# Where the clearing transfers of the experts' input stand in SP's queue of a graph-network kernel

## The reference

```python
cnt = cnt.at[dst, edge_type].add(1.0)
inv_deg = 1.0 / jnp.maximum(cnt[dst, edge_type], 1.0)
for l in range(DEPTH):                       # 4
    h = jnp.einsum('ni,rio->rno', X, W)
    msg = h[etype, src] * inv_deg[:, None]
    agg = jax.ops.segment_sum(msg, dst, num_segments=X.shape[0])
    out = agg + X @ root + bias
    ...
    X = jax.nn.elu(layernorm(out)) + X
...
top_vals, top_idx = jax.lax.top_k(logits, K) # K = 2 of 8 experts
```

## Time and profile before

| | |
|---|---|
| time, median of 3 runs | 2591.7 us (2585.16 to 2593.56) |
| the profiled execution's own time | 2582.19 us |
| its span in the trace | 2580.4 us |
| PE busy | 2099.1 us (81%) |
| DVE, ACT, POOL busy | 1564.4, 825.1, 1251.7 us |
| mean granted TensorE clock | 0.911 of full |
| DMA moved | 443.95 MB, mean 172 GB/s |

### The profile page before, as it was taken

The page is one execution under the profiler, slowest core; times in us unless marked ns, Lnnn a source line. Parts: engine busy times, 40 slices in busy tenths (PEclk is TensorE's granted clock), DMA queues, the critical chain, the costliest instruction groups (busy, mean ns, idle before and its releaser), DMA issues. The chain is left out here.

```text
span 2580.4 us, 46242 instructions
## 1 busy us (share of the span) xinstructions
PE 2099.1 (81%) x16341; PEld 1303.8 (51%) x16341; DVE 1564.4 (61%) x4433; ACT 825.1 (32%) x1679; POOL 1251.7 (49%) x1223
## 2 busy tenths in 40 slices
PE   2667788888789898989889888888897988774993
PEld 1334455555454454555545555555453554444992
DVE  7957666666575465666545565665364665565665
ACT  3645545445365111111111211111010111113992
POOL 2055443353510366666526666663656666642441
PEclk6688899899899999999989999999998999886997
DMA  6798343343433587676547877665775656532335
GB/s 150 176 289 249 122 132 108 111 133 116 126 89 130 185 238 227 216 220 193 180 123 260 236 235 221 213 213 171 223 228 162 179 174 179 152 94 64 93 96 178
DMA packets 211689, 443.95 MB, mean 172 GB/s; under 512 B 40881, under 2 KB 137150, under 8 KB 209795
## 3 DMA queue, kind: packets, MB, share of 16 engines
q1 hardware_dynamic: 138291, 273.04, 34.6%
q0 software_dynamic: 61408, 156.79, 20.6%
q10 hardware_dynamic: 11760, 11.08, 1.7%
HBM read 336.54 MB, written 103.89 MB: 171 GB/s over the span
## 5 line engine op out<-in xcount | busy, mean ns | idle before, releaser
L1446 POOL DMA_INDIRECT n_BIG<-n_xd,n_SIDX x1080 | 1111.2, 1029 | 1093.6 <-PE n_PS L1931 453.2
L1912 PE MATMUL n_PS<-n_BIG 125*128 125x500 f16 x4800 | 1187.7, 386 | 60.9 <-issue 33.9
L1912 PEld LDWEIGHTS n_PS<-n_BIG 125*128 125x128 f16 x4800 | 439.6, 100 | 500.4 <-issue 128.8
L1931 PEld LDWEIGHTS n_PS<-n_OW,n_BIG 128*128 128x128 f16 x4320 | 256.5, 99 | 198.3 <-issue 67.9
L1931 PE MATMUL n_PS<-n_OW,n_BIG 128*128 128x84 f16 (+21 forms) x4320 | 305.9, 202 | 53.2 <-issue 45.6
L1951 PE MATMUL n_PS<-n_BIG,n_tabs 128*128 128x256 f16 x2400 | 310.9, 284 | 32.8 <-issue 30.9
L1626 DVE TENSOR_TENSOR n_ST<-n_PS,n_INVB 128x500 f32<-128x500 f32 x200 | 200.2, 1043 | 158.8 <-remote 62.8
L1951 PEld LDWEIGHTS n_PS<-n_BIG,n_tabs 128*128 128x128 f16 x2400 | 243.3, 102 | 85.5 <-issue 48.6
L1652 DVE SCALAR_TENSOR_TENSOR n_U<-n_PS,n_cw,n_BI 125x256 f32<-125x256 f32 x100 | 48.3, 483 | 350.0 <-remote 194.7
L1337 ACT ACTIVATE n_tabs<-n_ST 128x1000 f16<-128x1000 f32 x100 | 103.8, 1038 | 383.8 <-DVE n_ST L1626 263.9
L1321 ACT ACTIVATE n_BIG<-n_PS 128x500 f16<-128x500 f32 x300 | 163.5, 577 | 189.5 <-PE n_PS L1883 122.6
(11 more groups left out here) (276 smaller groups left out, 2268.7 us busy)
## 6 DMA issues: line engine op xcount, KB each, us to landing
n_BIG<-n_a SPq DMA_DIRECT2D x175, 625.0 KB
n_a<-n_BIG SPq DMA_DIRECT2D x12, 3125.0 KB
n_xg<-n_tabs SPq DMA_DIRECT2D x53, 481.9 KB
n_INVB<-n_ind SPq DMA_DIRECT2D x100, 250.0 KB
n_BIG<-n_xd,n_SIDX POOLq DMA_INDIRECT x1080
n_BIG<-in_L_ffn_W_dram SPq DMA_DIRECT2D x32, 512.0 KB
n_xd<-n_BIG SPq DMA_DIRECT2D x75, 112.0 KB
n_whl<-n_BIG SPq DMA_DIRECT2D x16, 512.0 KB
```

What stands on the lines that cost most here:

```text
L1446: e.indirect_dma_start(m.GR[:, g % GS, :], None, m.XD[l % 2][:, :], bass.IndirectOffsetOnAxis(ap=m.SIDX[:, i:i + 1], axis=0)).then_inc(s[f ...
L1912: ins = e.matmul(m.bank(2 * p + h, 0, W), m.xps[l % 2][0:TN, part, D * k + 128 * h:D * k + 128 * h + 128], m.RA[0:TN, c.slot_of(n), W * (k ...
L1931: ins = e.matmul(m.bank(2 * p + h, at, c.width[q]), m.GR[:, g % GS, D * part + 128 * h:D * part + 128 * h + 128], ow, start=(first == 0 an ...
```

## The change

The 54 clearing transfers keep their size and their waits. Before, transfer n stands in SP's queue behind block n, so that all 54 stand behind blocks 0 to 53. Now transfer k stands behind block 50 + 4k, the first behind tile 1's last blocks, the last behind block 262 of 300.

```diff
--- before.py
+++ after.py
@@ -50,6 +50,7 @@
 ZROWS = 96
 ZN = 5
 N_ZERO = math.ceil((DUMMY + 128) / ZROWS / ZN)
+ZERO_FROM, ZERO_STEP = 50, 4
 ROWS = (0, 112), (112, TN)
 HEAD = 32
 SIGMA = 4.0
@@ -341,8 +342,8 @@
                 split_in[l] = run("dve", 3.0, run("act", 2.6)) + 0.3
             elif what == "block":
                 unit_ready["block", n] = run("act", 0.6) + 0.2
-                if n < N_ZERO:
-                    order.append(("zx", 0, n))
+                if n >= ZERO_FROM and (n - ZERO_FROM) % ZERO_STEP == 0 and (n - ZERO_FROM) // ZERO_STEP < N_ZERO:
+                    order.append(("zx", 0, (n - ZERO_FROM) // ZERO_STEP))
             elif what == "tile":
                 job(time["pe"] + 5.0, "degree", 0, n)
             elif what == "counts":
```

## The result

The changed kernel takes 2575.64 us (median of 8 runs, 2568.62 to 2587.94) where the kernel before takes 2589.61 us on the same chip (8 runs, 2585.16 to 2600.48). The ratio is 0.9949, with a 95% interval of 0.993 to 0.9968 (some 8 to 18 us): 14.0 us less, where 15.5 was forecast. The profiled execution took 2569.7 us, 12.5 less than the profiled one of before.

What follows compares the result with a forecast made beforehand. DVE sets the pace while tile 0 is built, then PE, which idles 13.88 us for tile 0's counts. Terms -13.9 - 1.2 - 1.4 + 1.0 = -15.5 us take the median from 2591.7 to 2576.2; range 2566 to 2588.

Steps and rivals of the forecast that it cites:

- Tile 0's counts: At PE's start on tile 0's degrees: the 13.88 us wait for the counts' transfer goes entirely, -13.9 us.
- Both delays of the counts: Before tile 0's degrees: 6.5 us in SP's queue, some 7.6 us behind bytes already handed to the DMA engines.
- What is late next: Behind tile 0's counts: DVE doesn't become the bound; POOL's gathers count nothing, with 5 us as far end.
- The clock: At the 16 products behind tile 0's degrees: 3.70 us at full clock instead of 4.90, -1.2 us.
- The late inverse: At 231 to 243 us, DVE's 3.37 us wait for an inverse goes; -1.4 us taken, bounds 0 and 3.4.
- Other idle time: PE from 160 to 215 us, 22% idle under DMA load: 0 us taken as gain, 3.3 kept as bound.
- The clears in their new place: From about 200 to 765 us, clears delay small transfers behind them in SP's queue: +1 us, bounds 0 and 8.
- a sign of its being wrong: PE's waits for counts, inverses or gathered rows appearing between 200 and 760 us would show the prediction wrong.
- Slower: Rival: clears in their new place delay what stands behind them, up to 93 us, unhidden; 2606 with a third; chance 0.04.
- The counts still land late: Rival: x's last halves and POOL's first gathers delay tile 0's counts instead of the clears; 2584 us, chance 0.12.
- More comes back: Rival: all bounds on the gaining side at once, 21.8 us, giving 2570 us; chance 0.08.
- The forecast DMA share of 0.57: From 240 to 760 us, the moved clears raise the DMA engines' share from 0.41 to 0.57.

Runs made afterwards that it cites:

- e3: The kernel before, with tile 0's counts sent from ACT's queue instead of SP's and all clears in their old place; ratio 1.0 to the kernel before.
- e5: The kernel before, unchanged, run once more on a chip where it takes 2277 us; one run, 2281.01 us.
- e12: The kernel before with 25 clears left behind blocks 0 to 24, the other 29 behind every fourth block from 50; ratio 1.0008 to the kernel before.
- e7: The changed kernel with all 54 clears behind blocks 246 to 299, one per block; ratio 1.0068 to the kernel before.
- e1: The changed kernel itself again, on a chip where the kernel before takes 2280 us; ratio 0.9869 to the kernel before.
- e2: The changed kernel with the clears behind blocks 25 to 78, one per block, beside tile 1; ratio 1.006 to the kernel before.
- e11: The changed kernel itself once more, on a chip where the kernel before takes 2280 us; ratio 0.9846 to the kernel before.
- e9: The changed kernel plus 54 transfers of 24.7 KB in the clears' old places; ratio 0.9866 to the kernel before.

## Why the prediction was right, and where it was not

- *Tile 0's counts, -13.9.* It measured 12.1 at D. The wait went entirely, but PE came 1.8 us later than assumed: 0.9 us later to the 12 products before, which then took 3.68 us instead of 2.69, at a granted clock of 0.75 (133 to 137 us; before 1.00). Both delays of the counts are real: past SP's queue D comes at 139.49 (e3) instead of 150.39 (e5), and the 7.3 us that the counts then take to land leave 3.17 us of wait. That this term gives the gain by itself is shown on no chip. e3 has it alone and gets 1.0; e12 leaves it out and gets 1.0008, which shows that it is needed on that chip, not that it is enough.
- *What is late next.* The prediction asked this, and named DVE's own work and POOL's gathers. The answer in e3 is the inverses, 15.47 and 17.05 us of DVE's waits. The sum was spared this only because the change moves the clears away from the inverses as well.
- *The clock, -1.2.* The 16 products took 3.54 us instead of 4.90, 1.4 less; the 12 products before them gave 1.0 back.
- *The late inverse, -1.4.* DVE's wait of 3.37 us is gone, and yet the lead over before, 13.5 us at the first gathered rows, is 9.2 at M, where the sum has it rise. 4.3 us are lost in between; one trace of each kernel on a chip with stops can't say to what. The bound of 3.4 was the mistake in method: it is the wait for the inverse that is left behind late counts, not what the inverse costs once the counts are early.
- *Other idle time, 0 with 3.3 as bound.* Nothing shows against it on the chip of the forecast (e12, and the window of 160 to 215 us). Elsewhere it is the largest mistake: DVE's 20.0 us for inverses in e5. The step that failed there is "No row of PE there names a transfer, so I take 0". PE's row names DVE, and DVE waits for the transfer; rows of SP with 12 clears in 20.63 us between two inverses were there to follow.
- *The clears in their new place, +1, bounds 0 and 8.* One wait of 1.47 us for tile 2's counts shows, between 200 and 760 us, where the prediction had put a sign of its being wrong. The lead of 9.2 us at M is 9.9 at the degrees of tile 11 (816.32 against 826.23), behind the last clear, so no larger loss is seen. On the faster chips e7 against e1 puts it at about 8. The forecast DMA share of 0.57 came out at 0.54.
- *The rivals.* "Slower" had a true mechanism, 1.68 us a clear, wherever clears stand in a row (e2, e7); the change keeps them four blocks apart in the list. "The counts still land late" did not come: behind early halves and gathers they were there in time. "More comes back", 21.8 us at most, was too small for the other chips, where e1 and e11 gained 31 to 35.

The time was forecast within 1.5 us, and some of that is luck. At the end of layer 0 the two traces stand 9.9 us apart, at their ends 12.5 (the last 2.6 where the change moves nothing), the medians 14.0 with an interval of 8 to 18. What the prediction had right is that the clears make the counts late in two ways, that this goes entirely, and that the clears cost little where they now stand. What it had wrong is that the counts are the gain: they are one of two delays, and early counts alone give nothing where that was tried (e3).

## What to carry to other kernels

Bulk transfers that nobody waits for still set the pace of small ones that somebody waits for; put them where the DMA engines are idle, or apart by more than their own time, and never in a row close ahead of a small one. Removing one late transfer of a row moves the wait to the next, so follow each releaser over a second and third hop and ask when the next hop would be ready if the first were early. The wait that the trace shows at the second hop is only what the first has left of it. And the same change was worth 14 us on one chip and 31 to 35 on two others, so compare within one chip, and say of which kind it was.

## What was not expected of the hardware

- The same kernel takes 2277 to 2280 us on three chips and 2586 to 2590 in two sets, at mean granted clocks of 0.934 and 0.911 for the profiled kernel before. For the changed kernel 199 of 321 us are idle time of PE, with 207 us of its waits put down to "issue" against 2; DVE is busy for as long (1565.4 and 1560.7 us). The cause stays open.
- A store of 2 KB on ACT's own queue took 10.2 us to land while SP's clears filled the DMA engines, and 2.1 us without them.
- SP issues a single clear in 0.42 us, with idle DMA engines (276.33 us in the changed kernel) and even right behind the save of a matrix (208.57). In a row of 17 a clear takes 1.68 us (e7), and four right behind such a save 16.94 together (e3), four transfers of 24.7 KB there 6.97 (e9): a few are taken at once, then SP stands still.
